# Four 64x64 mask products side by side in place of two of 128x128

## The reference

```python
bq = q.reshape(b, h, w, WINDOW, d) * QK_SCALE        # WINDOW = 64
bk, bv = look_around(k), look_around(v)              # the window before, and its own: 128 keys
sim = einsum('bhwid,bhwjd->bhwij', bq, bk)
mask = (i < j) | (i > j + WINDOW) | (j == -1)        # a band of 65 keys for each query
sim = where(mask, -finfo.max, sim)
out = softmax(sim) @ bv
```

## Time and profile before

| | us |
|---|---|
| runs: median (lowest to highest of 3) | 2464.89 (2462.02 to 2475.73) |
| profiled execution, its own time | 2463.41 |
| its span, first to last instruction | 2461.6 |
| TensorE, matmul busy | 2219.0 (90%), 20746 instructions |
| TensorE, weight loads busy | 1385.9 (56%) |
| VectorE busy | 1644.9 (67%) |
| ScalarE busy | 1589.0 (65%) |
| GpSimd busy | 562.6 (23%) |
| DMA engines, share | 15.6% of 16 engines on the main queue |

### The profile page before, as it was taken

One profiled execution on the slowest core, in us unless ns is written; L12 is line 12 of the kernel. 1 busy time (PEld: TensorE's weight loads), 2 busy tenths in 40 slices (PEclk: granted clock), 3 DMA queues, 4 the chain that ended last, 5 costly groups with the idle time before them and its releaser, 6 DMA issues. The chain is left out here.

```text
span 2461.6 us, 51938 instructions
## 1 busy us (share of the span) xinstructions
PE 2219.0 (90%) x20746; PEld 1385.9 (56%) x20746; DVE 1644.9 (67%) x2617; ACT 1589.0 (65%) x3047; POOL 562.6 (23%) x528
## 2 busy tenths in 40 slices
PE   3699998989999999998999989899899999999897
PEld 2455655546565466655565555565656556565454
DVE  2566675676866778667776677676776676866674
ACT  1367765667657676677666776666766767667664
POOL 2022230231302412024210243012330231302410
PEclk9899999999999999999999999999999999999998
DMA  4200132001320013201230012200122001320000
GB/s 109 57 2 17 36 53 42 10 8 36 57 38 17 5 39 60 29 16 29 38 59 6 16 32 57 38 6 17 32 57 42 17 1 32 53 38 17 16 17 25
DMA packets 62519, 78.60 MB, mean 32 GB/s; under 512 B 9266, under 2 KB 57132, under 8 KB 59948
## 3 DMA queue, kind: packets, MB, share of 16 engines
q1 hardware_dynamic: 62284, 75.29, 15.6%
HBM read 11.37 MB, written 4.19 MB: 6 GB/s over the span
## 5 line engine op out<-in xcount | busy, mean ns | idle before, releaser
L1007 POOL TENSOR_TENSOR pr<-pr 128x1024 f32<-128x1024 f32 x128 | 301.9, 2359 | 1006.7 <-DVE pr L908 1006.7
L870 DVE TENSOR_REDUCE nm<-ps 128x2 f32<-128x768 f32 (+3 forms) x384 | 387.6, 1042 | 113.5 <-PE ps L562 107.9
L803 ACT ACTIVATE pr<-ps,wb,inv 128x128 f32<-128x128 f32 x1024 | 369.6, 477 | 130.2 <-DVE wb L925 130.0
L505 PE MATMUL ps<-cf,pr 128*128 128x128 f32 x2048 | 285.0, 280 | 73.7 <-POOL pr L1017 52.5
L760 ACT ACTIVATE pr<-ps 128x896 f32<-128x896 f32 x256 | 233.9, 918 | 124.5 <-PE ps L580 123.0
L505 PEld LDWEIGHTS ps<-cf,pr 128*128 128x128 f32 x2048 | 224.8, 141 | 133.9 <-POOL pr L1017 64.8
L901 DVE TENSOR_TENSOR pr<-ps,rot 128x1024 f32<-128x1024 f32 x128 | 156.5, 1223 | 141.0 <-ACT pr L775 131.6
L919 DVE TENSOR_REDUCE wm<-ps 128x8 f32<-128x1024 f32 x128 | 156.7, 1224 | 116.6 <-PE ps L657 114.2
L580 PE MATMUL ps<-Q,K 128*128 128x512 bf16 (+3 forms) x1024 | 227.0, 303 | 0.0
L579 PE MATMUL ps<-cb 128*128 128x128 bf16 x1024 | 198.4, 221 | 31.3 <-DMA Q<-mT 19.3
L561 PE MATMUL ps<-K,Q 128*128 128x128 bf16 x1024 | 195.9, 222 | 25.2 <-DMA K<-Kf 20.3
(11 more groups left out here) (151 smaller groups left out, 4349.5 us busy)
## 6 DMA issues: line engine op xcount, KB each, us to landing
pr<-V SPq DMA_DIRECT2D x32, 520.0 KB, 4.5
Q<-Kf SPq DMA_DIRECT2D x224, 64.0 KB
K<-Kf SPq DMA_DIRECT2D x224, 64.0 KB
pr<-V SPq DMA_DIRECT2D x32, 390.0 KB, 6.0
xn<-in_L_attn_x SPq DMA_DIRECT2D x16, 256.0 KB, 2.8
out<-hT SPq DMA_DIRECT2D x16, 256.0 KB, 2.2
Q<-in_c_edge SPq DMA_DIRECT2D x32, 64.0 KB
Q<-mT SPq DMA_DIRECT2D x128, 4.0 KB
```

Source lines behind the costliest of these rows:

```text
L505: mm = pe.transpose(dst[:, t * P:(t + 1) * P], src(t), ident)
L803: ins = act.activation(P2[s][:, 2 * (p % 2) + r, o:o + P], bank[:, r * T + o:r * T + o + P], ACT.Exp, scale=inv[s][:, t, h:h + 1], bias=wb ...
L870: dve.tensor_reduce(nm[s][:, qt, h0:h0 + n], src, AX_X, ALU.max, negate=True).then_inc(nm_r[s], 1)
L1007: pool.tensor_tensor(t1[s][t % 3], t1[s][t % 3], t2[s], ALU.add).then_inc(sum_r[s], 1)
```

## The change

The two mask products of a pair (identity 128x128, 512 columns, one for each head) become four, one for each head `r` and each window `half`: a 64x64 block of the identity, times 64 rows of the band constant, into 64 rows of a bank. They use the same rows of the array and the same rows of the output as the score products behind them. The band constant becomes 640 columns wide with both halves alike; `half` 0 reads it from column 0, where the first 64 columns are all masked, and `half` 1 from column 128. The strings `ALL` and `FIRST_BANKS` are new throughout, so steps of the even and odd elements are woven in another order and banks are assigned anew. The list of steps of one element, the semaphores and all the other instructions stay.

```diff
-ALL = ("3230000022a69208202ba3b6db76fffbb90b54805494abcc...
+ALL = ("00000055a84e1b040115cab6edb6fffad463cc888494cbcd...
...
-FIRST_BANKS = ("010101023042600162040232043240604620445425064200...
+FIRST_BANKS = ("010102304260016024062767204670240624001021402640...
...
-        cb = sb("cb", [P, 3 * P + T], BF16)
+        cb = sb("cb", [P, 4 * P + T], BF16)
         identb, causal, causal_t = (cb[:, i * P:(i + 1) * P] for i in range(3))
-        band_q = cb[:, 3 * P:3 * P + T]
+        band_q = [cb[:, 3 * P + i * P:3 * P + i * P + T] for i in range(2)]
...
-                        for r in range(2):
-                            pe.matmul(bank[:, r * T:(r + 1) * T], identb, band_q, start=True, stop=False,
-                                      skip_group_check=True)
+                        for half in range(2):
+                            for r in range(2):
+                                rows = slice(D2 * r, D2 * r + D2)
+                                pe.matmul(bank[D2 * half:D2 * half + D2, r * T:(r + 1) * T], identb[rows, rows],
+                                          band_q[half][rows, :], start=True, stop=False, skip_group_check=True)
...
-    band_q = np.tile(np.where(in_band, 0.0, MASKED), (1, NT))
-    band_q[:D2, :D2] = MASKED
-    same, before = c % D2 >= i, c % D2 <= i
+    band_q = np.tile(np.where(in_band, 0.0, MASKED), (1, NT + 1))
+    band_q[:, :D2] = MASKED
```

More of the change, by code:

```diff
@@ L88, in steps @@
     return between + [(0, name) for name in out[:cut]]
[L94 to L99, removed]
+ALL = ("00000055a84e1b040115cab6edb6fffad463cc888494cbcd11bfbb4424452bb9c12bfaad9c1020444b5572adbaedbffead18f3222125"
+       "2af3446fded109112adcf049fbae6b04081112b55cab6eb6efffab4636c890294abd5133efb4424452b75c127f5e4dc10204452e572a"
+       "dbadbbffead18f32211252af3446fded109114b6e704af9beab04081112755ccb6eb6efffad463cc888494abcc91bf7b4424452db9c1"
+       "33f5ed4c1020445365732dbaedbffead18f322092532f3246feed109114b6e7049fb6d6704081112975ccb6ebb6fffab4a36c850494c"
+       "bd491bf7b442444ad75c12bf6d71c10204451d572adbadbbffead18f322212533b9446fbed0892192bddc68569d50ed56b1a07b2ddd5"
+       "00a483c057f8a759c7f95e92a53ab88d9ddfffffc")
 def merged():
@@ L116 @@
 ORDER = merged()
[L119 to L144, removed]
@@ new lines @@
+FIRST_BANKS = ("010102304260016024062767204670240624001021402640260420102146024602460410642064206406704162046024034602301612"
+       "604064206467267460724672604076061260123640260124130216014532536723672362362326324356746524506140106104512014"
+       "506410236234504523674235263240254635401201564523423572362745673263273423423623452456472367236723476206204236"
+       "230140167230164016234012640310142601264026402301206124602406320132063232601624062406240210426042604204502140"
+       "264026036402301412406046204645245640562456402054041640167420640162170614012376374564754654564546542354324362"
+       "304120104102316012304210674672302367452345362340354625401201564523423572362745673263232632632432672674567545"
+       "764576254604602674670126017450142015462015642010126401642064206701604162406204760176047676401462046204620610"
+       "264026402602306120642146026402301612604064206467267460742674602076061402654026406742754670546723420132013012"
+       "302320325342352405462746762764570674562476012014504576237236243270267436701201645423523472367254327632372432"
+       "432632452456475467546754276406402456450120167450147650274067243234260432064026402301206124602406320132063267"
+       "201264026402640610462046204604506140624126046204501614602062406267467260724672604076061260123640260124130216"
+       "014532456327632732362326324352342564502140102106714016702610452456706745236237243260276437601201745423523462"
+       "372654763273263423423623452456472367236723476206204236230142301670362376041064250454026410642064206701604162"
+       "406204760176047674601742064206420410246024602402304120462164024602301412406046204645245640526452406054041240"
+       "123460240126130214016732734523452342342324326372362746702160102104516014502410672674504567234235263240254635"
+       "401201564523423572362745673263273423423623452456472367236723476206204016012342367012307162071406124010142601"
+       "264026402301206124602406320132063267201264026402640610462046204604506140624062072406701416402042604245645240"
+       "526452406054041240123460240126130214016732674325432532342324326374564726704160104102316012304210674672302367"
+       "452367342360376427601201745423542367236745672362372432432632452456472367236723476206204236230142301670134210"
+       "634012640310142601264026402301206124602406320132063232630423046204620610264026402602306120642064074206701216"
+       "204024602423623420346234624030120162476204624560576234230173674235423523243234236274564726704160104102316012"
+       "304210674672302367452345362340354625401201564523423572362745673263232632632432672674567545764576254604602674"
+       "670120145670156021470124603245026410642064206701604162406204760176047646501462046204620610264026402602306120"
+       "642146026402301612604064206467267460742674602076061460145620460142150416012354356745674564564546542356746543"
+       "026320412014506104512401672674506745234235263240254635401250461021301012031302103203203230237467016237210321"
+       "036230236746701201302103232323102310")
```

## The result

The changed kernel takes 2430.06 us (median of 4 runs, 2427.62 to 2436.17) against 2463.45 for the kernel before, measured beside it: a ratio of 0.986, 95% interval 0.9832 to 0.9889. It is faster by 33 us, where 24 were forecast. Measured a second time it was 2427.03, with a ratio of 0.9846 (0.9814 to 0.9879). Its profiled execution took 2427.62 us, with a span of 2425.8.

The account below looks back on a forecast made before the run. TensorE's stream was taken to bound the kernel: 27.8 us of masks plus 4.1 of shape changes, less 8 returning as waits, is 24 off 2463.4; with 1.5 for the median, 2441 us, range 2424 to 2463.

Parts of the forecast that it names:

- Four at once: In each wscore step the four bf16 mask products run together, one 0.217 us round in place of two: 27.8 us less.
- Rivals 2 and 3: Mask products: either two rounds as now, about 2461 us, chance 0.05; or all four in a row, 2516, chance 0.04.
- Change of shape, 0.09 each: Each switch of TensorE between full array and quarters costs 0.09 us; 44 fewer switches save 4.1 us.
- The stream's sum, 31.9: Work leaving TensorE's stream: 27.8 us of mask rounds plus 4.1 us of shape changes.
- The difference of the open weight loads: First weights after a shape change, now a mask's not a score's: taken as zero, bounds ±4.5 us over 128 steps.
- What comes back, 8: Part of the gain returning as TensorE waits for ACT's exponentials and POOL's scaled keys: 8 us, a quarter; bounds 0 to 27.8.
- Rival 1: The exponentials take over: every mask round gained turns into waiting, about 2461 us; half of it, 2448; chance 0.11 in full.
- The new order, 0: Effect of the new weave on TensorE's holes, 138.8 us in the steady part: some tenth either way, taken as zero.
- Rival 4: New banks: 95 extra early returns to a bank each wait 0.4 us for a reader, 38 us back, 2479; chance 0.06.

Follow-up runs that it names:

- a plain rule: Changed kernel with each bank, or neighbouring two, chosen as the one whose last taking lies farthest back, in place of the written digits: 2554.63 us, ratio 1.0367.

## Why the prediction was right, and where it was not

The time came out 11 us below the forecast of 2441, and within its range. That it did is in part luck: of the 24 us forecast from the masks they brought 14.5, and the new order, taken at zero, brought 22.

- **Four at once: right.** Rivals 2 and 3 fall with 0.24 us from the first mask to the first score. So the trace decides against the Trainium skill's sentence in "TensorE: Matmul & The Clock Gate", Part 3, "What overlaps and what doesn't", that a weight load overlaps running products only in another row group. Here four loads of two row groups take 0.11 us together, and loads for all four places begin at 784.48 while products run in all four.
- **Change of shape, 0.09 each: right.** 0.20 from a transpose to the mask (784.45 − 784.25), of which 0.11 is the transpose's own columns, and 0.08 between masks and scores where the columns change (0.32 − 0.24).
- **The stream's sum, 31.9: too small.** 29.3 us of work went in 96 steps; mine would be 23.9. The difference of the open weight loads, set to zero with ±0.035 us a step as bounds, is at the favourable bound: the step itself is 0.35 shorter and 0.09 more stands ahead of it, 0.25 net where 0.217 was predicted. And a `wscore` behind another overlaps with it: 0.55 less, where 0.22 + 2 x 0.09 = 0.40 were predicted.
- **What comes back, 8: the step that failed.** With the order held, 14.3 of 28.2 us of work became idle time in 12 of 16 elements, and with the new order 13.5 of 30.7: half, where I took a quarter. I bounded each hole's growth by one mask round and by the mean mask time in front of POOL's chain; a step shrinks by 0.25 to 0.55, and L805 and L1019 together grew by 12.6 us in the old order, over the bound of 9.9. The sum behind it also set a chain of 4.1 us against TensorE's 4.01 for a pair. The 4.1 is DVE's 1.22 and ACT's 2.9 one behind the other; for the next pair each engine is free after its own part, so this does not show that ACT is the slower. Rival 1 was half true in its number: its half-way price, 2448 (2447 by its own terms), is near what the masks alone gave, 2450. Which chains hold the time back stays open.
- **The new order, 0: wrong by 22.** I compared medians of distances. They say nothing on seven single late steps; the row was there, 19.3 us in seven waits for `Q<-mT`, and it is in no term of the sum. What the order does to each wait of that list would have been the question.
- **The clock: missing.** The kernel before lost 20.5 us to it in the stretch of its trace. A hole can cost its own length and, behind it, a stretch at the lower clock.
- **Rival 4: not here,** though banks are far from harmless. With the 95 more early returns no wait of masks or `wctx` for the exponentials appears; a plain rule brings such waits, and costs 125 us.

## What to carry to other kernels

Small products that write to quarters of the array belong beside those that follow in the same quarters: the masks' second round goes, and so does the change of shape between steps that meet. Where TensorE is 90% busy and each engine follows one list, don't count all that leaves the stream as time; here it was half. Go through the list of waits by the longest single wait, DMA queues included: two 4 KB transfers that queued behind 28 of 64 KB, once for each pair of elements, cost 23.5 us of time, and 39 us less of products brought 14.5. Two remedies ended this wait, an earlier place in the queue and other work put ahead of the step that waits. Test a new order and a new instruction apart. And compare the granted clock of all runs before you explain a few microseconds from one trace.

## What the runs showed of the hardware

Two steps of 64x64 products in a row overlap: masks of the second start with the first's last scores (1137.78 and 1137.81 above). A change of shape costs about 0.09 us, also where only the columns change (0.32 against 0.24 us from mask to score).

In the kernel before, TensorE's wait of 6.65 us until 407.95 goes with a granted clock of 0.51 from 406 to 413; where that hole was closed it was 1.00. Three more of the waits for `Q<-mT`, of 2.42, 2.98 and 4.0 us, have the lower clock right behind them:

```profile
706.00:710.00 4.00, 3.87 (x8) 1.95 (x9) 0.00 (x0) 2.81 (x3) 0.00 (x0) 0.57 0.00 0
1293.50:1297.00 3.50, 3.26 (x7) 1.67 (x8) 0.00 (x0) 2.01 (x2) 0.00 (x0) 0.52 0.00 0
1590.40:1593.80 3.40, 3.40 (x7) 1.74 (x6) 0.00 (x0) 2.67 (x3) 0.00 (x0) 0.51 0.00 0
```

Two of 1.26 and 1.33 us (at 1005.6 and 2183.6) have not: the clock is 1.00 in the 5 to 6 us behind them. The clock's loss of one kernel varies from run to run by some 20 us of 2460 (37 to 59 in 35 runs of the kernel before). Closing the waits for `Q<-mT` moved its median from 49 to 39.
